# Weight tables of a language-model tower on one core: two products for each table instead of three, in another order

## The reference, cut to what matters

```
# token layer (8 heads of 64)
Q = layer_norm(tok, gamma, beta) @ W_proj.T        # 192 -> 512
V = tok @ W_val.T
traces = 0.99 * (value_traces - erase) + 0.1 * v_update
h = shifted(Q) @ traces  (per head)  @ W_out.T     # -> 192
# attention layer, on x1 = layernorm(h)
q, k, v = split(x1 @ W_qkv + b_qkv)
scores = (q @ k.T) * scale * group_weight          # group_weight from softmax(gelu(v @ W_gp))
out = weights @ v @ W_proj + b_proj
# feed-forward layer: 64 soft-routed experts of 16 slots
```

## Time and profile before

| what | us |
|---|---|
| median of 3 runs (459.14 to 460.05) | 459.62 |
| the profiled execution | 457.82 |
| its span, from which all rows are taken | 456.0 |
| front stretch, last grams to first mixed tile (67.45 to 84.09) | 16.64 |
| ramp, first mixed tile to first value product (84.09 to 91.89) | 7.80 |

### The profile page before, as it was taken

How to read it: one execution, slowest core, us unless ns; L and a number is a source line. 1 busy time by engine, 2 the same in 40 slices (tenths; PEclk the granted TensorE clock), 3 DMA queues, 4 the chain that set the end, 5 groups by cost and what they waited for, 6 DMA issues and landing times.

```text
span 456.0 us, 8360 instructions
## 1 busy us (share of the span) xinstructions
PE 432.1 (95%) x3114; PEld 357.1 (78%) x3114; DVE 297.5 (65%) x779; ACT 228.1 (50%) x415; POOL 141.8 (31%) x235
## 2 busy tenths in 40 slices
PE   7898998998999999989999999999999899999995
PEld 5666666798788887878888888899975587787895
DVE  6799882486766657767777668766875253453564
ACT  5566742598833644744322557888864312122220
POOL 5666700375100007620003491013631331211310
PEclk9999999999999999999999999999999999999999
DMA  2115300200100000500000000004539999999404
GB/s 89 43 46 161 115 2 0 105 1 2 30 0 1 0 1 0 201 9 1 0 0 1 2 0 1 1 1 183 234 130 418 379 354 381 388 367 378 169 19 138
DMA packets 14231, 49.64 MB, mean 109 GB/s; under 512 B 3504, under 2 KB 8528, under 8 KB 9968
## 3 DMA queue, kind: packets, MB, share of 16 engines
q1 hardware_dynamic: 7584, 43.21, 25.3%
q0 software_dynamic: 2912, 3.37, 2.6%
q10 hardware_dynamic: 3696, 2.54, 1.8%
HBM read 45.94 MB, written 3.15 MB: 108 GB/s over the span
## 4 chain that ended last, share of the span: by engine, by line
PE 64%; DVE 13%; DMA 12%; POOL 4%; ACT 3%; issue 3%; SPq 0%; ACTq 0%; POOLq 0%; DVEq 0%
DMA w1r<-in_p_w 11%; PE ps L924 8%; PE ps L970 8%; PE ps L1126 5%; PE ps L1067 3%; PE ps L904 2%; PE ps L1096 2%; PE ps L950 2%; PE ps L951 2%; PE ps L952 2%; PE ps L954 2%; PE ps L953 2%; PE ps L1113 2%; DVE qw L1601 2%; DVE ss L1591 1%
## 5 line engine op out<-in xcount | busy, mean ns | idle before, releaser
L924 PE MATMUL ps<-pr,et 128*128 128x192 f32 x256 | 46.2, 331 | 1.6 <-DVE et L1790 1.2
L1126 PE MATMUL ps<-ys,ct 128*128 128x192 f32 x256 | 45.2, 330 | 0.7 <-DMA ys<-ys_dram 0.7
L1965 DVE TENSOR_TENSOR res<-ps,res 128x384 f32<-128x384 f32 x64 | 35.7, 558 | 14.2 <-PE ps L1126 9.7
L924 PEld LDWEIGHTS ps<-pr,et 128*128 128x128 f32 x256 | 41.2, 189 | 4.5 <-ACT et L1349 2.7
L1126 PEld LDWEIGHTS ps<-ys,ct 128*128 128x128 f32 x256 | 41.2, 190 | 4.1 <-issue 2.7
L590 POOL DMA_DIRECT2D ys<-ys_dram x32 | 19.7, 619 | 69.2 <-DMA ys_dram<-ysb 68.0
L1465 ACT ACTIVATE hs<-ps 128x384 f32<-128x384 f32 x16 | 7.8, 490 | 57.9 <-PE ps L1067 57.9
L506 POOL TENSOR_SCALAR ve<-mv 128x1 f32<-128x1 f32 x32 | 10.1, 314 | 81.7 <-DVE mv L1805 41.4
L1338 ACT ACTIVATE scs<-ps,pr 128x1024 f32<-128x1024 f32 x16 | 17.8, 1114 | 29.9 <-PE ps L872 29.9
L1956 DVE COPY ysb<-ps 128x192 f32<-128x192 f32 x16 | 5.7, 357 | 39.5 <-PE ps L1096 39.5
L1342 ACT ACTIVATE zz<-zz,nmx 128x1024 f32<-128x1024 f32 x16 | 18.4, 1151 | 26.0 <-DVE nmx L1784 25.8
(11 more groups left out here) (315 smaller groups left out, 1189.5 us busy)
## 6 DMA issues: line engine op xcount, KB each, us to landing
w1r<-in_p_w SPq DMA_DIRECT2D x16, 1152.0 KB, 19.4
w2r<-in_p_w SPq DMA_DIRECT2D x16, 1152.0 KB, 19.3
ys_dram<-ysb ACTq DMA_DIRECT2D x16, 96.0 KB, 8.7
ys<-ys_dram POOLq DMA_DIRECT2D x32, 48.0 KB, 7.2
phT<-in_p_phi SPq DMA_DIRECT2D x1, 1024.0 KB, 4.7
wT<-in_p_qkv SPq DMA_DIRECT2D x1, 774.0 KB, 5.8
out<-res SPq DMA_DIRECT2D x3, 192.0 KB, 3.4
out<-res ACTq DMA_DIRECT2D x3, 192.0 KB, 3.8
```

What stands on the lines that cost most here:

```text
L924: last = mm(d[:, 0:D], et[:, k, :], pr[:, b * KT + k, 1:1 + D], start=(k == 0), stop=(k == KT - 1))
L1126: last = mm(bank(5 + q % 3)[:, h * D:(h + 1) * D], ct[:, u % 2, k + h, :], ys[:, t % YR, b, :], start=True, stop=True)
L1965: v.tensor_tensor(res[:, i:i + 2, :], bank(5 + q % 3)[:, 0:2 * D].rearrange("p (h d) -> p h d", h=2), res[:, i:i + 2, :], ALU.add).then_in ...
```

## The change

Each table now has two products, A (128 columns of weights) and B (66). For B, ScalarE rounds the 66 rows into B2, waits for that, and copies B2's partitions 0 to 63 to B1's partitions 0 to 63. VectorE writes B1's partitions 64 to 127, reading the PSUM bank and B2 at partitions 0 to 63, and then the remainder of B2's bias row. The list SETUP is beta, kB, nA, nB, kA, vA, vB. kB stands where kB1 stood, kA behind the n products; the copy to wpn no longer stands behind kB2's conversion, but follows the ones products by a wait of its own (mix_done 3) and counts on mm_ready. In the mixed loop, vA and vB stand at s = 0 and 1, and ScalarE and VectorE convert kA, vA, vB at the head of steps 1, 2 and 3.

```diff
-    CB1, CB2 = P, P + DB
+    CB2 = P + DB
...
-        SETUP = ["beta", "kA", "kB1", "kB2", "nB2", "nB1", "nA", "vA", "vB1", "vB2"]
-        SETUP_BANK = [7, 7, 6, 7, 6, 4, 5, 5, 6, 5]
+        SETUP = ["beta", "kB", "nA", "nB", "kA", "vA", "vB"]
+        SETUP_BANK = [7, 6, 5, 4, 7, 6, 5]
         at = {n: k for k, n in enumerate(SETUP)}
-        PARTS = {"A": (0, P), "B1": (CB1, P), "B2": (CB2, DB + 2)}
+        PARTS = {"A": (0, P), "B": (CB2, DB + 2)}
+        HI = [n + part for n in SETUP for part in (("", "+") if n[1] == "B" else ("",))]
+        hi_at = {n: k for k, n in enumerate(HI)}
...
-            prepare("kA", 1)
-
             pe.wait_ge(m["in_mix"], 16 * 5)
             pe.wait_ge(m["bs_ready"], 2)
...
-            prepare("kB1", 0)
+            prepare("kB", 0)
 
             pe.wait_ge(m["tt_ready"], 1)
...
-            pe.wait_ge(m["setup_taken"], at["kA"] + 1)
+            pe.wait_ge(m["setup_taken"], at["beta"] + 1)
             for t in range(HP):
-                mm(setup_bank("kB2")[:, 272 + 2 * t:274 + 2 * t], wpT[DB:DB + 1, 1, t * P:(t + 1) * P],
-                   ones[DB:DB + 1, 0:2], start=True, stop=True)
-            prepare("kB2", at["kA"] + 1)
-
-            pe.wait_ge(m["mm_ready"], 2)
-            pe.wait_ge(m["setup_taken"], at["kB2"] + 1)
-            for name, free in (("nB2", at["kB1"] + 1), ("nB1", 0), ("nA", 0)):
+                last = mm(bank(7)[:, 2 * t:2 * t + 2], wpT[DB:DB + 1, 1, t * P:(t + 1) * P], ones[DB:DB + 1, 0:2],
+                          start=True, stop=True)
+            last.then_inc(m["mix_done"], 1)
+
+            pe.wait_ge(m["mm_ready"], 3)
+            for name in ("nA", "nB"):
...
-            pe.wait_ge(m["setup_taken"], at["nA"] + 1)
+            prepare("kA", 0)
+            pe.wait_ge(m["setup_taken"], at["nB"] + 1)
+            pe.wait_ge(m["setup_hi"], hi_at["nB+"] + 1)
             pe.wait_ge(m["wn_ready"], NB)
...
+                if i == 3:
+                    pe.wait_ge(m["setup_taken"], at["kA"] + 1)
...
                 if s == 1:
-                    prepare("vB1", 0)
+                    prepare("vB", 0)
...
-                if s == 3:
-                    prepare("vB2", at["vA"] + 1)
...
-                elif part == "B1":
-                    last = sc.activation(B1, d[:, 0:n], ACT.Copy, scale=scale[1])
                 else:
-                    last = sc.activation(B2, d[0:DB + 2, 0:n], ACT.Copy, scale=scale[2])
-                last.then_inc(m["setup_hi"], 1)
+                    sc.activation(B2, d[0:DB + 2, 0:n], ACT.Copy, scale=scale[1]).then_inc(m["setup_hi"], 1)
+                    act.wait_ge(m["setup_hi"], hi_at[name] + 1)
+                    sc.copy(B1[0:DB], B2[0:DB].bitcast(F32)).then_inc(m["setup_hi"], 1)
...
-                elif part == "B1":
-                    last = remainder(B1[DB:P, :], d[DB:P, 0:n], scale[1], B1[DB:P, :])
                 else:
+                    v.scalar_tensor_tensor(B1[DB:P], d[0:DB, 0:n], scale[1], f(B2[0:DB]), ALU.mult, ALU.subtract)
                     last = remainder(B2[DB:DB + 1, :], d[DB:DB + 1, 0:n], scale[2], B2[DB:DB + 1, :])
-                if name == "kB2":
-                    last = v.tensor_copy(wpn[:, :, XC:PC], d[:, 272:272 + 2 * HP].rearrange("p (t c) -> p t c", c=2))
...
-            round_k("kB2")
-            for name in SETUP[4:7]:
+            dve.wait_ge(m["mix_done"], 3)
+            v.tensor_copy(wpn[:, :, XC:PC], bank(7)[:, 0:2 * HP].rearrange("p (t c) -> p t c", c=2)).then_inc(m["mm_ready"], 1)
+            for name in ("nA", "nB"):
                 round_n(name)
...
-                if s in (1, 2, 4):
-                    round_v({1: "vA", 2: "vB1", 4: "vB2"}[s])
+                if s == 1:
+                    round_k("kA")
+                if s in (2, 3):
+                    round_v({2: "vA", 3: "vB"}[s])
```

More of the change, by code:

```diff
@@ L1198, in round_up @@
                 d = setup_bank(name)
-                part = name[1:]
-                if part == "A":
-                    last = sc.activation(Ah, d[:, 0:n], ACT.Copy, scale=scale[0])
-                elif part == "B1":
-                    last = sc.activation(B1, d[:, 0:n], ACT.Copy, scale=scale[1])
-                else:
-                    last = sc.activation(B2, d[0:DB + 2, 0:n], ACT.Copy, scale=scale[2])
-                last.then_inc(m["setup_hi"], 1)
+                if name[1:] == "A":
+                    sc.activation(Ah, d[:, 0:n], ACT.Copy, scale=scale[0]).then_inc(m["setup_hi"], 1)
+                else:
+                    sc.activation(B2, d[0:DB + 2, 0:n], ACT.Copy, scale=scale[1]).then_inc(m["setup_hi"], 1)
+                    act.wait_ge(m["setup_hi"], hi_at[name] + 1)
+                    sc.copy(B1[0:DB], B2[0:DB].bitcast(F32)).then_inc(m["setup_hi"], 1)
             def round_k(name):
                 Ah, _, B1, B2 = (t[:, 0:XC + 1] for t in kv)
-                round_up(name, (SCALE, SCALE, SCALE), Ah, B1, B2, XC + 1)
+                round_up(name, (SCALE, SCALE), Ah, B1, B2, XC + 1)
             def round_v(name):
                 Ah, _, B1, B2 = (t[:, XC + 1:KV] for t in kv)
-                round_up(name, (1.0, 1.0, 1.0), Ah, B1, B2, D + G)
+                round_up(name, (1.0, 1.0), Ah, B1, B2, D + G)
             def round_n(name):
-                round_up(name, (gamA, gamB, gamR[0:DB + 2]), nAh[:], nB1[:], nB2[:], D)
+                round_up(name, (gamA, gamR[0:DB + 2]), nAh[:], nB1[:], nB2[:], D)
             sc.dma_start(cols[:], a["p_cols"]).then_inc(m["in_tok"], 16)
@@ L1521, in round_off @@
             def round_off(name, scale, Ah, Al, B1, B2, n):
[L1523 removed]
+                dve.wait_ge(m["setup_hi"], hi_at[name] + 1)
                 d = setup_bank(name)
[L1525 to L1526 removed]
+                if name[1:] == "A":
                     last = remainder(Al, d[:, 0:n], scale[0], Ah)
[L1528 to L1529 removed]
                 else:
+                    v.scalar_tensor_tensor(B1[DB:P], d[0:DB, 0:n], scale[1], f(B2[0:DB]), ALU.mult, ALU.subtract)
                     last = remainder(B2[DB:DB + 1, :], d[DB:DB + 1, 0:n], scale[2], B2[DB:DB + 1, :])
[L1532 to L1533 removed]
                 last.then_inc(m["setup_taken"], 1)
@@ L1542, in round_n @@
             def round_n(name):
-                round_off(name, (gamA, gamB[DB:P], gamR[DB:DB + 1]), nAh[:], nAl[:], nB1[:], nB2[:], D)
+                round_off(name, (gamA, gamB[0:DB], gamR[DB:DB + 1]), nAh[:], nAl[:], nB1[:], nB2[:], D)
             def stats(i):
@@ L1657, in _ @@
             v.tensor_tensor(tt[DT:P], traces(1)[DT:P], tt[DT:P], ALU.add).then_inc(m["tt_ready"], 1)
-            round_k("kB1")
+            round_k("kB")
             dve.wait_ge(m["mix_done"], 2)
             v.tensor_copy(mm_[:, 1:HP:2, :], bank(3).rearrange("p (t c) -> p t c", t=2)[:, :, 0:D]).then_inc(m["mm_ready"], 1)
-            round_k("kB2")
-            for name in SETUP[4:7]:
+            dve.wait_ge(m["mix_done"], 3)
+            v.tensor_copy(wpn[:, :, XC:PC], bank(7)[:, 0:2 * HP].rearrange("p (t c) -> p t c", c=2)).then_inc(m["mm_ready"], 1)
+            for name in ("nA", "nB"):
                 round_n(name)
```

10 lines of the change are left out of this document (3 added, 7 removed).

## The result

The changed kernel took 453.01 us (median of 4 runs, 452.55 to 453.86), the kernel before 459.84 us beside it (4 runs, 459.14 to 463.39): ratio 0.9881, 95% interval 0.9842 to 0.992. The ratio isn't the quotient of these two medians, which is 0.985. The sign is as forecast. So something was mis-sized by more than I allowed for. The trace says at once that it isn't the stretch that the change touches.

The account below looks back on a forecast made before the run. The prediction took a serial string of small TensorE products as the bound. Front terms 1.26 + 0.10 + 2.05 + 1.30 - 0.42 = 4.29, plus 0.1 in the ramp, made 4.4 us: 459.62 to 455.2 us, range 453.9 to 456.5.

Parts of the forecast that it names:

- (1): Ahead of the update products: the kA product leaves, moving all that follows forward by 1.26 us.
- (2): In front of the mix: the product is 66 columns wide, not 128, saving 0.10 us.
- (3): Between ones and n products: kB2's product goes and the wpn copy follows directly, saving 2.05 us.
- Rival C: The wpn copy isn't earlier, held by VectorE work, losing at most 0.86 us: 456.1 us; chance 0.15 together with Rival B.
- (4): At the n products: one of three goes, saving 1.30 us.
- (5): Before the first mixed tile: a second VectorE instruction on nB adds 0.42 us; kA's product is hidden.
- The unseen cost: VectorE reading partitions 0 to 63 and writing 64 to 127: between 0.42 and 0.84 us, taken as 0.42.
- Rival B: Conversions across the partition halves cost 0.84 us each, leaving a gain of 3.6 us: 456.1 us; chance 0.15 together with Rival C.
- The ramp: Start of the mixed loop: a v product of 1.21 us goes, but only about 0.1 us arrives.
- Rival A: In the mixed loop's ramp TensorE sets the pace, so the whole 1.21 us arrives: 5.5 us gained, 454.1 us; chance 0.11.
- rival D: Mixed tiles miss the steady pace, 1.87 us apart and not 1.33: slower, 461.1 us; chance 0.02.
- The median: Over the whole kernel: the change takes 4.4 us off the runs' median of 459.62, giving 455.2 us.

Follow-up runs that it names:

- kA_front: The changed kernel with the kA product and its conversions put back ahead of the update products: 454.34 us, ratio 0.9914.
- split_n: The changed kernel with finer waits: nA's product waits for mm alone, the first mixed tile for nA, its fourth matmul for nB: 452.82 us, ratio 0.9876.
- wpn_alone: The kernel before, three products per table kept, with the wpn copy given its own wait ahead of kB2's conversions: 456.34 us, ratio 0.9963.
- kA_twice: The changed kernel with kA's two matmuls made once more, for nothing, ahead of the real ones: 454.24 us, ratio 0.991.
- after: The changed kernel itself, in its first measurement and profile: 453.01 us, ratio 0.9881.
- v_three: The changed kernel with its v table made by three products, as before the change: 453.38 us, ratio 0.9883.
- vB_late: The changed kernel with vB converted at the head of step 4 of the mixed loop, not 3: 453.39 us, ratio 0.9883.
- again: The changed kernel, unaltered, measured once more beside the kernel before: 453.2 us, ratio 0.9879.
- null: The kernel before, unaltered, measured against itself: 457.74 us, ratio 0.9991.
- after_wait: The changed kernel with two useless VectorE instructions ahead of the wpn copy, so TensorE waits longer before the n products: 454.81 us, ratio 0.9907.

## Why the prediction was right, and where it was not

**The starting point** (a serial string of small products, almost wholly on TensorE, nothing to hide behind) held: kA_front gives 1.26 us for 1.26 us of work, and split_n's 0.7 us arrives in full at the last x1t.

**(1) and (2), kA and the narrower product.** Forecast 1.26 + 0.10. The mix starts 6.62 us behind r1 before and 5.26 after: 1.36. The mix at 72.39 is earlier than the 72.9 named, only because r1 was 0.55 us early.

**(3) The wpn copy.** Forecast 2.05. From the start of the ones products to the first n product, by the timeline: 3.36 us before (75.68 to 79.04), 1.30 after (73.77 to 75.07), so 2.06. The short wait was put at 0.26 and is 0.25 (73.83 + 0.99 to 75.07). VectorE was free in time, as argued. Rival C falls with that. wpn_alone shows that over half of the term came from the wait alone.

**(4) One n product.** Forecast 1.30, measured 1.22 (4.10 us of TensorE before, 2.88 after). I had taken the distance of the conversions of the middle product and the last one; what went is a little less than that. This is the largest miss of the front sum, 0.08 us.

**(5) The end.** Forecast +0.42. From ScalarE's nB to M0 it is 1.34 us, 0.93 before: +0.41. M0 is released by VectorE's second instruction on nB, as forecast; kA's product ends at 79.00 (78.30 + 0.70), 0.32 us before M0, and kA_twice puts its cover at 0.39 (forecast 0.4). The rows after (TensorE, ScalarE):

```profile
78.30 0.70 PE L624 MATMUL ps<-wT 64*128 64x257 f32 x2
79.32 0.36 PE L604 MATMUL ps<-nAh,XH 128*128 128x192 f32 x1 [0.32 <-DVE nB L1519]
```

```profile
78.43 0.35 ACT L1206 CAST nB<-nB 64x192 fp32r<-64x192 f32 x1
```

**The front** sums to 4.23 us against 4.29.

**The unseen cost.** VectorE from partitions 0 to 63 into 64 to 127 took 0.41 us (78.43), the lower bound of 0.42 to 0.84 and the value that I took. Rival B falls. ScalarE's copy between two SBUF tiles took 0.35, less than the 0.42 to 0.84 given. The pair on nB takes 0.84 us (78.43 to 79.27) with no overlap (0.42 from start to start, 0.41 long), so the rule weighed there (the Trainium skill, "VectorE: DVE Perf Modes", section "Two Vector instructions with no wait between them") gave the right one of the two sums; it decided 0.09 us.

**The ramp.** Forecast: of the v product's 1.21 us about 0.1 arrives, x1t of tile 4 at 9.56 from M0. Measured 9.57, with tile 3's statistics at 6.03 (forecast 6.05). The rest of it is TensorE waiting. In after (the pair on vB, tile 3's statistics, TensorE's wait, x1t of tiles 4 and 5):

```profile
84.49 0.40 DVE L1528 SCALAR_TENSOR_TENSOR kvB<-ps,kvB 64x241 fp32r<-64x241 f32 x1
...
84.91 0.41 DVE L1519 SCALAR_TENSOR_TENSOR kvB<-ps,kvB 1x241 fp32r<-1x241 f32 x1
...
85.35 0.37 DVE L1702 BATCH_NORM_STATS2 st<-ps 128x6 f32<-128x192 f32 x1
...
86.70 0.32 PE L780 MATMUL ps<-ident,x1t 128*128 128x128 f32 x1 [0.71 <-ACT x1t L1301]
...
88.89 0.51 ACT L1300 ACTIVATE x1t<-ps,nmr,rstd 128x192 f32<-128x192 f32 x1 [0.26 <-POOL nmr L514]
...
90.22 0.51 ACT L1300 ACTIVATE x1t<-ps,nmr,rstd 128x192 f32<-128x192 f32 x1
```

TensorE's wait of 0.71 us and one of 0.19 behind it are the "about 1 us in sum". Rival A falls by v_three. The pace is 1.33 us (88.89 to 90.22), so rival D falls too. The working of the ramp was right in the main but would have misled as a guide: it names tile 3's statistics as the link, and vB_late shows that freeing them moves the work to the next tile's, for 0.19 us where 0.4 was expected.

**The sum of the trace.** Forecast 4.4 us, to the last x1t measured 4.28 to 4.33 (after, again). "All later stages 4.4 us earlier" was too simple for the end of the kernel, since the wait for w1r scatters by over 2 us of its own.

**The median, and the step that failed.** "The median of the runs is 459.62, 1.8 us more than the profiled one; the change takes the same off it." I took the 1.8 us as scatter or as something outside the stretch, which both kernels would have. That term was wrong: the changed kernel's median of ten (453.19) doesn't lie 1.8 us above its two profiled executions, it lies under both (453.86 and 453.23). The 1.8 us of before were most likely the clock fall, but no profile of these executions shows it. The three (459.14 to 460.05) all lie in the later group of the table, whereas the profiled one, 457.82 with a clock of 1.00, lies in the earlier. The change removes the wait of 1.16 us behind which null's clock falls, and of the changed kernel and its variants none shows a fall there but after_wait, which puts the wait back and leaves it unfilled. Between the earlier group and the changed kernel the difference is 457.5 - 453.2 = 4.3 us, the forecast's 4.4; between the three given and the changed kernel it is 6.4. Set against the profiled execution's own time my sum gave 453.4, which is 0.2 from the median of ten. The size of the gap between the profiled execution and the median, next to a range of runs of only 0.9 us, should have been a term of its own, with the wait that the change removes as a place to look.

## What to carry to other kernels

Where a serial string of small products bounds a stretch, it can be summed from the trace to a tenth of a microsecond, and the cheapest gain is often a short copy that stands behind work it doesn't need (1.2 of 4.3 us here). Where another engine's chain sets the pace, removed work turns into waits even if the engine was busy all the time (1.2 us removed, under 0.1 seen). When the profiled execution and the median of the runs differ by more than the runs do among themselves, find out what differs before carrying the gap over unchanged: it may hang on the very wait that the change removes.

## What was unexpected of the hardware

TensorE's granted clock went from 1.00 to 0.50 behind a wait of only 1.16 us (null) and of 1.08 us (after_wait), inside a stretch in which it was otherwise busy with small matmuls, and came back some 3 us later; it cost 1.44 and 1.68 us, more than the wait itself. It doesn't happen in each execution: the profile of before has the same wait and no fall, and kA_front has none behind 1.38 us. The falls near the start (wpn_alone, after_wait) show no cost beyond the scatter: r1 comes at 67.69 and 67.11 there, and at 66.99 to 67.61 in the twelve profiles without one. What decides whether the clock falls stays open. That the mean clock also counts a fall at the very end, where it costs nothing, can be one reason for the lower mean clock of the nine shorter executions of the kernel before; no profile shows it for them.
